# A two-layer gated transformer block on one core: the last stage cut into two token halves, one of them worked among the attention heads

## What is computed

```python
x = x + tanh(g_xattn[1]) * attention(layernorm(x), ctx, Wq, Wk, Wv, Wo)
x = x + tanh(g_ffn[1]) * ffn(layernorm(x))
# ffn: 32 experts, latent width 128, shared width 512
scores = sigmoid(x @ gate_w.T)                    # T x 32
sb = scores + gate_bias
# of 4 groups of 8, keep the 2 whose two best sb sum highest; then the top 8
wsel = scores[top 8]; wsel = wsel / wsel.sum() * 2.5      # cw: T x 32
x_lat = x @ fc1_w.T                               # T x 128
h = relu(x_lat @ w1[e].T) ** 2 * cw[:, e]         # each expert, all tokens
routed = sum_e(h @ w2[e].T) @ fc2_w.T
shared = relu(x @ shared_up_w.T) ** 2 @ shared_down_w.T
```

## Time and profile before

| | us |
|---|---|
| three runs | 610.44, 615.82, 616.7 (median 615.82) |
| the profiled execution, own time | 612.76 |
| its span in the trace | 611.0 |
| outside the span | 1.8 |
| busy: PE, DVE, ACT, POOL | 548.5, 398.0, 362.3, 338.3 |

### The profile page before, as it was taken

How to read it: one execution, slowest core, us unless ns; L and a number is a source line. 1 busy time by engine, 2 the same in 40 slices (tenths; PEclk the granted TensorE clock), 3 DMA queues, 4 the chain that set the end, 5 groups by cost and what they waited for, 6 DMA issues and landing times.

```text
span 611.0 us, 9318 instructions
## 1 busy us (share of the span) xinstructions
PE 548.5 (90%) x3210; PEld 467.5 (77%) x3210; DVE 398.0 (65%) x786; ACT 362.3 (59%) x689; POOL 338.3 (55%) x285
## 2 busy tenths in 40 slices
PE   1999878998988999999999899999957948999995
PEld 1778656777777999999999899999945747777773
DVE  5868868689775444444454645666677576888884
ACT  2642233656567777677676666877722904767672
POOL 1687346598164776766556645677525621554440
PEclk9999989999988999999999999999996969999999
DMA  7611227100343556544444333323030007776732
GB/s 258 231 53 51 104 86 234 61 35 18 95 148 119 162 169 179 148 156 134 126 156 139 109 98 105 87 70 87 18 104 1 2 6 275 235 237 230 243 125 70
DMA packets 55070, 75.84 MB, mean 124 GB/s; under 512 B 5488, under 2 KB 34416, under 8 KB 55024
## 3 DMA queue, kind: packets, MB, share of 16 engines
q1 hardware_dynamic: 55024, 75.24, 38.6%
HBM read 57.27 MB, written 17.96 MB: 123 GB/s over the span
## 4 chain that ended last, share of the span: by engine, by line
PE 74%; DVE 16%; ACT 5%; issue 2%; DMA 1%; POOL 1%; SPq 0%; DVEq 0%; ACTq 0%
PE ps L1221 21%; PE ps L1223 20%; PE ps L1222 20%; PE ps L1312 4%; PE ps L1414 2%; PE ps L1398 2%; DVE ln_y L871 1%; DVE h L881 1%; DMA cT_raw<-in_ctx_t 1%; PE ps L1421 1%; DVE ln_t L869 1%; ACT q2T L732 1%; PE ps L1427 1%; PE ps L1235 1%; DVE st L851 1%
## 5 line engine op out<-in xcount | busy, mean ns | idle before, releaser
L572 POOL TENSOR_TENSOR probs<-probs,rsum 128x512 f32<-128x512 f32 x64 | 66.8, 1043 | 81.6 <-DVE rsum L1008 81.6
L1003 DVE TENSOR_REDUCE nmax<-ps 128x2 f32<-128x512 f32 x64 | 44.1, 689 | 42.0 <-PE ps L1223 40.8
L658 ACT ACTIVATE kv_out<-ps 128x512 f32<-128x512 f32 x64 | 38.5, 601 | 45.8 <-PE ps L1223 45.7
L769 ACT ACTIVATE probs<-ps,nmax 128x256 f32<-128x256 f32 x128 | 59.5, 474 | 4.9 <-DVE nmax L1003 4.9
L994 DVE TENSOR_TENSOR pT_lo<-ps,pT_hi 128x512 fp32r<-128x512 f32 x64 | 44.3, 691 | 25.4 <-ACT pT_hi L775 24.2
L833 ACT ACTIVATE e_hi<-e_r 128x1024 fp32r<-128x1024 f32 x32 | 34.0, 1062 | 34.6 <-PE ps L1223 24.6
L501 POOL TENSOR_TENSOR w_hi<-w_raw,zeros 128x256 fp32r<-128x256 f32 x32 | 20.1, 628 | 59.6 <-PE ps L1223 38.4
L507 POOL TENSOR_TENSOR kv_w_lo<-blk_raw,kv_w_hi 128x1024 fp32r<-128x1024 f32 x15 | 37.4, 2494 | 24.6 <-ACT kv_w_hi L650 24.6
L775 ACT ACTIVATE pT_hi<-ps 128x512 fp32r<-128x512 f32 x64 | 38.4, 600 | 21.2 <-PE ps L1312 21.2
L999 DVE TENSOR_TENSOR oT_lo<-ps,oT_hi 128x512 fp32r<-128x512 f32 x32 | 22.1, 692 | 40.7 <-ACT oT_hi L779 40.7
L1188 DVE SCALAR_TENSOR_TENSOR e_r<-ps,cw_row 128x1024 f32<-128x1024 f32 x32 | 39.2, 1224 | 14.0 <-PE ps L1223 14.0
(11 more groups left out here) (245 smaller groups left out, 1892.8 us busy)
## 6 DMA issues: line engine op xcount, KB each, us to landing
cw_row<-cw_scratch SPq DMA_DIRECT2D x32, 512.0 KB, 4.9
blk_raw<-in_w_blocks SPq DMA_DIRECT2D x23, 512.0 KB, 3.7
k_scratch<-kv_out SPq DMA_DIRECT2D x32, 256.0 KB, 2.2
v_scratch<-kv_out SPq DMA_DIRECT2D x32, 256.0 KB, 2.4
k_raw<-k_scratch SPq DMA_DIRECT2D x32, 256.0 KB, 2.8
v_raw<-v_scratch SPq DMA_DIRECT2D x32, 256.0 KB, 2.6
w_raw<-in_w_t SPq DMA_DIRECT2D x32, 128.0 KB, 4.7
xr<-in_x SPq DMA_DIRECT2D x2, 512.0 KB, 6.3
```

The source lines that it names most:

```text
L572: nc.gpsimd.tensor_tensor(probs[:, b, :, :], probs[:, b, :, :], rsum[:, b, :].unsqueeze(2).to_broadcast([P, 2, S]), ALU.mult).then_inc(pro ...
L769: last = nc.scalar.activation(probs[:, b, t, :], ps[:, S_BANK[b], t * S:(t + 1) * S], ACT.Exp, bias=nmax[:, b, t:t + 1], accum_out=esum[:, ...
L1003: V.tensor_reduce(nmax[:, b, :], ps[:, S_BANK[b], :].rearrange("p (t k) -> p t k", t=2), AX.X, ALU.max, negate=True).then_inc(max_done, 1)
```

## The change

**Halves.** Tokens 0 to 511 are finished by attention after step 17. Their LayerNorm, router, latent and shared up projection now run in the attention steps of the second half. DVE has the LayerNorm at the ends of steps 19, 20 and 21, the router at the ends of 25 to 29; PE has its parts as tasks, in the fill places that are empty from step 21 on (`TASK_IN_STEP`), of which each is one bank: N now in two chunks, L with tokens as the stationary side (24 matmuls of 32 columns instead of 6 of 512), X, four U, C (the turn of cw). The scores' sigmoid becomes an Exp on ACT and an add and a reciprocal on DVE, so B goes.

**Experts.** 64 half units i: first all 32 experts for half 0, then for half 1. `up` and `down` are three matmuls of 512 columns each; up(i+4) is issued ahead of down(i), with four PSUM banks. ACT writes the full square to SBUF (`e_sq`), and the subtraction e_sq minus e_hi is by POOL in three units of four (first half) or every second (second half), by DVE in the others. `cw_row` is 256 KB per half unit. The expert weights are loaded once, as eight blocks of 512 KB, into the places of attention weights that are done, and kept for both halves; POOL and ACT split them by `block_low` and `block_high`, three during attention and five at units 0, 4, 8, 12 and 16.

**Second half.** Its LayerNorm (units 2 to 4), its tasks (`TASK_IN_UNIT`), its router (DVE, units 11 to 19) and the shared down projections of half 0 (units 3, 5, 7, 9) stand inside the unit loop; the shared down of half 1 at units 40 to 46. fc2 of half 0 goes at unit 36 and its store soon after; the end has only half 1 left.

The core of the diff:

```diff
+        TASK_IN_STEP = {"m22": ("N", 0), "e22": ("N", 1), "e23": ("L", 0), "m24": ("X", 0), "e24": ("U", 0), "m25": ("U", 1),
+                        "e25": ("U", 2), "m26": ("U", 3), "m30": ("C", 0)}
+        TASK_IN_UNIT = {6: ("N", 0), 8: ("N", 1), 10: ("L", 0), 11: ("X", 0), 13: ("U", 0), 14: ("U", 1), 15: ("U", 2), 16: ("U", 3),
+                        20: ("C", 0)}
+        STEP_OF_BLOCK = {..., 22: 23, 24: 24, 27: 25, 29: 26, 31: 27}
+        UNIT_OF_BLOCK = {0: 28, 4: 29, 8: 30, 12: 31, 16: 32}
+        def low_on_pool(i):
+            return i % 4 != 3 if i < E else i % 2 == 0
 # SP
+            def load_row(i):
+                g, e = i // E, i % E
+                if i >= 4:
+                    sp.wait_ge(root_done, i - 3)
+                sp.dma_start(cw_row[i % 4][:, :], cw_scratch[e:e + 1, g * GT:(g + 1) * GT].broadcast_to([P, GT])).then_inc(ld_cw[i % 4], 16)
 # POOL
             for u in range(NU):
...
                 normalise(u, 1)
+                if u == 25:
+                    shared_low(0)
+                    shared_low(1)
+                elif u == 26:
+                    shared_low(2)
+                elif u == 27:
+                    shared_low(3)
                 if u + 2 < NU:
                     key_low(u + 2)
                 if u in STEP_OF_BLOCK:
                     block_low(STEP_OF_BLOCK[u])
+            def expert_low(i):
+                if i >= NI or not low_on_pool(i):
+                    return
+                pool.wait_ge(e_sq_done, i + 1)
+                if i >= 4:
+                    pool.wait_ge(down_done, i - 3)
+                nc.gpsimd.tensor_tensor(e_lo[i % 4][:, :], e_sq[i % 2][:, :], e_hi[i % 4][:, :].bitcast(F32), ALU.subtract)\
+                    .then_inc(low_by_pool, 1)
+            for i in range(NI):
+                expert_low(i + 3)
+                if 15 <= i < 15 + SC:
+                    shared_low(SC + i - 15)
+                if i in UNIT_OF_BLOCK:
+                    block_low(UNIT_OF_BLOCK[i])
 # ACT
+            def expert_square(i):
+                act.wait_ge(root_done, i + 1)
+                if i >= 4:
+                    act.wait_ge(down_done, i - 3)
+                nc.scalar.activation(e_hi[i % 4][:, :], e_r[i % 2][:, :], ACT.Square).then_inc(e_hi_done, 1)
+                if i >= 2:
+                    k = i - 2
+                    act.wait_ge(low_by_pool if low_on_pool(k) else low_by_dve, lows(k, low_on_pool(k)))
+                nc.scalar.activation(e_sq[i % 2][:, :], e_r[i % 2][:, :], ACT.Square).then_inc(e_sq_done, 1)
 # DVE, at the end of step u
+                elif u == 19:
+                    factors_begin(0, GN)
+                    newton(0, GN, 1)
+                elif u == 20:
+                    newton(0, GN, 2)
+                elif u == 21:
+                    scaled(0).then_inc(h_ready, 1)
...
+                elif u == 25:
+                    shared_relu(2, 0)
+                    scores_of_groups(0)
+                elif u == 26:
+                    ranks_of_groups()
+                    scores_of_chosen_groups()
+                elif u == 27:
+                    choose_experts()
+                elif u == 28:
+                    weights_of_experts()
+                    roots_begin()
+                elif u == 29:
+                    roots_step()
+                    roots_step()
+                    roots_step()
+                    roots_end()
 # DVE, the unit loop
+            for i in range(NI):
+                root(i + 3)
+                expert_low(i + 2)
+                if i == 0:
+                    add_attention(GN)
+                elif i == 1:
+                    add_attention(GN + 2)
+                elif i == 2:
+                    factors_begin(GN, NT)
+                elif i == 3:
+                    newton(GN, NT, 2)
+                elif i == 4:
+                    newton(GN, NT, 1)
+                    scaled(1).then_inc(h_ready, 1)
...
+                elif i == 17:
+                    shared_relu(SC + 3, 1)
+                    roots_begin()
+                    roots_step()
 # PE, output of a head: the bank of a task must be free
                 if fills("m" + str(u + 1)):
                     pe.wait_ge(kv_taken, fills("m" + str(u + 1))[-1] + 1)
+                elif "m" + str(u + 1) in TASK_IN_STEP:
+                    wait_taken(0, TASK_IN_STEP["m" + str(u + 1)])
 # PE, the unit loop
+            for i in range(NI):
+                if i in TASK_IN_UNIT:
+                    if task:
+                        wait_taken(1, task)
+                    else:
+                        pe.wait_ge(o_done, NU)
+                    task = TASK_IN_UNIT[i]
+                    do_task(1, task, 1)
+                if i in SHARED_DOWN:
+                    shared_down(*SHARED_DOWN[i])
+                if i == E + 4:
+                    routed_out(0, 0)
+                    routed_out(0, 1)
+                up(i + 4)
+                down(i)
```

More of the change, by code:

```diff
@@ new lines, in flamingo_two_layer_kernel @@
+        keep(*kv_w_hi, *kv_w_lo)
+        xl_hi, xl_lo = [None] * NG, [None] * NG
+        xl_hi[0] = sb("xl_hi0", [P, GT], F32R, region)
+        xl_lo[0] = sb("xl_lo0", [P, GT], F32R, region)
+        s_sq = sb("s_sq", [P, 2, GT], F32, region)
+        keep(*blk_raw, wq_hi[1], wq_lo[1])
+        cw_row = [sb(f"cw_row{i}", [P, GT], F32, region) for i in range(4)]
+        keep(wq_hi[0], wq_lo[0])
+        router = ExitStack()
+        sc = sb("sc", [P, GN, E], F32, router)
+        sbias = sb("sbias", [P, GN, E], F32, router)
@@ L530, in _ @@
                 nc.gpsimd.tensor_scalar(wq8[i][:, :], wraw[i][:, :], -ROUND, 1.0, ALU.add, ALU.mult).then_inc(w_ternary, 1)
+            nc.gpsimd.memset(before[:, :, :], 0.0).then_inc(set_up, 1)
+            pool.wait_ge(set_up, 3)
+            for a in range(1, NGRP):
+                last = nc.gpsimd.memset(before[:, a, 0:a], 1.0)
+            last.then_inc(set_up, 1)
             pool.wait_ge(ld_small, 64)
@@ L839, in _ @@
+            act.wait_ge(down_done, NI)
+            for half in range(2):
+                s = slice(half * 2 * P, (half + 1) * 2 * P)
+                nc.scalar.activation(yl[1][:, s], ps[:, 1, s], ACT.Copy).then_inc(yl_done, 1)
         @block.vector
@@ L1213, in _ @@
+            for n in range(GN, NT):
+                add_result(n)
         @block.tensor
@@ new lines, in step_task, with open_banks @@
+            def step_task(key):
+                if key in TASK_IN_STEP:
+                    u = int(key[1:])
+                    if key[0] == "e":
+                        pe.wait_ge(q_done, min(u + 3, NU))
+                    else:
+                        pe.wait_ge(o_done, u - 1)
+                    do_task(0, TASK_IN_STEP[key], 1 if key[0] == "m" else 0)
+            def open_banks(banks):
+                for b in banks:
+                    mm(ps[:, b, :], zeros[:, 0:P], zeros[:, :], start=True, stop=False, skip_group_check=True)
@@ L1486, in _, with routed_out @@
+            def routed_out(g, half):
+                pe.wait_ge(yl_done, 2 * g + half + 1)
+                for n in (2 * half, 2 * half + 1):
+                    last = mm(ps[:, Y_BANK[half], n % 2 * D:(n % 2 + 1) * D], yl[g][:, n * P:(n + 1) * P], fc2[:, :], start=False,
+                              stop=(n % 2 == 1), skip_group_check=True)
+                last.then_inc(y4_filled, 1)
             for u in range(NU + 2):
```

783 lines of the change are left out of this document (413 added, 370 removed).

## The result

| | us |
|---|---|
| changed kernel, median of 4 runs | 631.61 (630.36 to 633.32) |
| kernel before, 4 runs beside it | 616.26 (610.44 to 618.5) |
| ratio, 95% interval | 1.028 (1.023 to 1.033) |
| span of the profiled execution | 629.5 (611.0 before) |

The changed kernel is 2.8% slower. 608 was forecast, and 631.6 lies above the range, 592 to 627. The whole loss shows in the windows of the changed kernel, cut at the first task (N, step 22), at steps 22 to 28, at the end of attention, at C of half 1 (unit 20) and at the last unit; the columns are those of the earlier trace rows.

The account below looks back on a forecast made before the run. PE was taken to bound the head steps and nearly the experts, waiting for DVE between them. Without waits 584.0 us, plus 15 of waits in attention and 9 in the unit loop, gave 608, range 592 to 627.

Parts of the forecast that it names:

- The end: After the unit loop: half of yl, fc2 of four tiles, adds, store and hand-overs, 7.0 us against 9.1 before.
- The time without waits, 584: Whole kernel if PE never waited: span 582.2 us, own time 584.0 with the 1.8 outside.
- The mechanism of the waits: In attention and units 0 to 19, SBUF-to-SBUF DVE instructions wait for POOL's running one; PE then waits, 2.7 to 6.3 at C.
- a value between the bounds: Waits taken as 15 us in attention (bounds 8 to 22) and 9 in the unit loop (3 to 19).
- Attention was put at 15: Attention steps 22 to 31: PE's waits behind DVE's bursts, plus up to 5 for the clock; 8 to 22 us.
- Units 0 to 20 were put at 9: Unit loop before C of half 1: PE waits for late DVE and POOL, 3 to 19 us including clock.
- 16 as the worst: Unit 20: with every burst between POOL's instructions, cw comes at 61 us, 16 late, before 3 for the clock.
- 53 us of POOL and of DVE's share: Units 0 to 19: POOL needs 37 us and DVE's 48 SBUF instructions 16 of the same ports, beside PE's 45.
- up to 5 and 3: Loss to PE's clock falling after waits: up to 5 us in attention, 3 more in the unit loop.
- The rival "POOL and DVE hold each other": Step 29's burst with C, and units 13 to 20: waits at upper ends, 22 and 19, total 625 us; chance 0.25.
- The third rival: Unit loop: cw_row's 256 KB per 1.40 us sets the pace, some 0.2 us per unit, total 621 us; chance 0.05.
- The second: Attention and unit loop: waits near lower ends, 8 and 3 us, since DVE has slack, total 595 us; chance 0.27.

Follow-up runs that it names:

- the best version: The changed kernel with ReLUs on ACT, POOL's low parts delayed in attention, half 1's tasks wider, last block's low part at unit 19, xl_lo before the scores: 610.98 us, ratio 0.992.
- the ReLU run: Against the changed kernel, ACT instead of DVE does the ReLUs of the shared units, with their squares at once: 629.94 us, ratio 1.027.
- POOL held: Against the changed kernel with ReLUs on ACT, POOL's low parts in steps 21 and 25 to 29 wait until DVE's burst is done: 623.64 us, ratio 1.017.
- the wide loop: Against the changed kernel with ReLUs on ACT, half 1's tasks at units 8 to 24, router pieces one per unit, ACT storing cwT: 626.22 us, ratio 1.021.
- the last three: The best version (610.98 us); that with C of half 0 at the end of step 30 (611.15); and that with half 1's logits also split (611.73).
- all three: Against the changed kernel, ReLUs on ACT, POOL's low parts delayed in attention steps, and half 1's tasks placed wider: 618.27 us, ratio 1.007.

## Why the prediction was wrong

**What bounds the kernel before, and PE's work after: right.** 45 us of PE for units 0 to 20 (45.27 measured with POOL cut), 38 of DVE (37.95), 67 for what comes behind C (67.8), logits at 0.11 us each. The end was put at 7.0 us and is 5.5. The time without waits, 584, stands as far as these parts go; attention without waits was never run.

**The mechanism of the waits: right.** An instruction from SBUF to SBUF waits for POOL's, one with a PSUM operand doesn't; C is where PE waits longest, twice; units behind C are at 1.40 us. This case's traces agree with the rule of the Trainium skill ("SBUF — State Buffer", Who interferes with whom) in two parts: DVE is held for the whole of POOL's instruction (1.01, 1.23 and 2.31 us), and not beside a POOL instruction that only writes (0.29 us beside the memsets).

**What failed is the choice of a value between the bounds,** "the ends don't add: while PE waits for one late thing, DVE and POOL catch up". Two terms rest on it. Attention was put at 15 and cost 24.4, above its own upper end of 22. Units 0 to 20 were put at 9 and cost 23.6, above their end of 19. Both upper ends, 41 us together, were too low for the 48 that were lost, and values near the middle were further off still. The runs show three reasons.

First, DVE and POOL don't catch up while PE waits, since they are what is late, and each holds the other. In units 0 to 20 PE's named waits alone are 18.1 us (cw 8.5, the ReLUs 5.3, h 3.7, two small ones), where I had 16 as the worst. I had the number, 53 us of POOL and of DVE's share beside 45 of PE, and took 9 us for a difference of 8 as if the two would interlock without a gap. By hand-placed bursts they did not, and 17 us go when POOL's low parts are cut. Yet the sum was no bound either: placed wider, nearly the same holds cost 13.9 us less. I priced how much work there was, and the loss was set by where it stood.

Second, the upper end was no end. It took POOL's instructions where they stood in the kernel before. Late bursts make late sums, and so the second probs and v_lo slide into the next burst: three holds at step 29, not two. And ReLU and pT_lo, with PSUM operands, were free of holds but queued behind instructions that weren't: PE waits 3.8 us on a ReLU in step 26 for which the prediction had 1.0 to 2.2, and 5.3 us on ReLUs in the units, where it named none. The other places of attention came out near their bounds: step 22 3.1 (1.9 to 2.6), steps 24 and 25 0.8 each (0.7), 27 0.5 (0.9 to 2.9), 28 and 29 0.7 and 1.4 (0.2 to 1.1), C in step 30 6.45 (2.7 to 6.3).

Third, the clock. Named waits are 19.2 us of attention's 24.4 and 18.1 of the units' 23.6, so some 5 us in each stretch are something else. In the units it is PE's own time: busy 50.52 us at a mean grant of 0.90, and 45.27 at 0.99 with POOL's low parts cut. I had up to 5 and 3. In attention the grant is 0.91 in its second part; that its 5 us are the clock too is likely and not shown.

The rival "POOL and DVE hold each other" is what happened, at its price of 625 and 6 us beyond. The third rival, cw_row as the pace, is excluded: units behind C take 1.40 us with a median of 3.4 us per row. The second, waits near the lower ends, was not reached by any order tried: the best version still has 97.3 us in attention, 7.4 less than the changed kernel.

How the 24.4 us of attention split is less clear than for the units. Holding POOL gives 5.8 and leaving out the router 10.5, of which the 5.8 are in part the same us. The rest (the LayerNorm in step 22, X, the tasks' hand-overs and the clock) was not taken apart.

## What to carry to other kernels

Before work is moved beside a full engine, list for each engine that serves it the instructions that read SBUF on both of DVE and POOL at the same time, and price each meeting at the whole of the other's instruction; if the sum of both comes near the time of the full engine, take the upper end, not the middle. Then ask for each meeting what the full engine waits for behind it: a held instruction costs time only in front of such a place. Such a meeting can be avoided without removing work: let POOL wait for the instruction behind DVE's burst (6.3 us for one wait in each of six steps), and give a chain of small instructions one place per unit. When a wait goes and the time stays, look at who comes late next: here cw, the ReLU and pT_lo were three names for one late DVE.

## What the runs showed that I had not expected

POOL is held too: 1.75 us for an e_lo of 1.30, behind a DVE subtraction from SBUF that had itself waited. A late engine so makes the other late.

The clock fell straight behind small matmuls. In the changed kernel 24 logits matmuls of 32 columns run from 514.92 to 517.5 us, 0.11 apart, and straight behind them matmuls of 512 columns come 0.43 apart (half speed, 1.2 GHz) until 521.5, then 0.23:

```profile
517.40 0.26 PE L1387 MATMUL ps<-gw_hi,hT_hi 128*128 128x32 f32 x1
517.51 0.48 PE L1385 MATMUL ps<-xl_hi,wq_lo 128*128 128x512 f32 x1
...
519.39 0.63 PE L1387 MATMUL ps<-e_hi,wo_hi 128*128 128x512 f32 x1
519.82 0.63 PE L1385 MATMUL ps<-hT_hi,fc_lo 128*128 128x512 f32 x1
```

Seven of the twelve traces of the changed kernel and its variants have such a stretch within the first six matmuls behind these logits, and all twelve have the 24 (the last one in two halves). PE's long wait before them is that for N of half 1: in six of the seven (the changed kernel, C of half 1 at unit 26, POOL cut in the heads, no router, the ReLU run, POOL held) PE had stood 3.7 us there. The five without the stretch (POOL cut in the units, the wide loop, the last three) had no wait over 1.4 us there, but neither had "all three", which has the stretch. So the small matmuls may have a part in it and aren't enough alone, nor is the wait needed; what decides stays open. It costs about 1.7 us (8 matmuls at 0.43 in place of 0.23).
